# Part of VectorE's attention work moved to GpSimd, and weight loads re-timed, in a transformer-block kernel

## The reference, cut to what matters

```python
x = x + layernorm(attn(layernorm(x)))          # per head: q, k scaled to unit length
#   sim = (l2norm(q) * exp(scale)) @ l2norm(k).T; out = softmax(sim) @ v; out @ w_out + b_out
x = x + layernorm(ffn(layernorm(x)))
#   h = silu(x @ w1 * s1) * (x @ w2 * s2); h = gelu(h @ h1 * t1); h = gelu(h @ h2 * t2); h @ w3 * s3
```

## Time and profile before

| | |
|---|---|
| median of 3 runs | 1945.36 us (1936.95 to 1945.42) |
| the profiled execution | 1939.09 us, of which the span is 1937.2 us |
| TensorE, VectorE, ScalarE, GpSimd busy | 1743.2, 1203.1, 1012.1, 426.7 us |
| mean granted TensorE clock | 0.966 of full speed |

### The profile page before, as it was taken

How to read it: one execution, slowest core, us unless ns; L and a number is a source line. 1 busy time by engine, 2 the same in 40 slices (tenths; PEclk the granted TensorE clock), 3 DMA queues, 4 the chain that set the end, 5 groups by cost and what they waited for, 6 DMA issues and landing times.

```text
span 1937.2 us, 24570 instructions
## 1 busy us (share of the span) xinstructions
PE 1743.2 (90%) x8584; PEld 1443.8 (75%) x8584; DVE 1203.1 (62%) x2085; ACT 1012.1 (52%) x1349; POOL 426.7 (22%) x499
## 2 busy tenths in 40 slices
PE   4899899999899889989988984699999999999997
PEld 3677777778678778777777773587878778777876
DVE  4676786786686776776776765664443544444453
ACT  2776676777677667767766763213232331313231
POOL 3333423423323423333333320000000000000000
PEclk8999999999999999999999997799999999999999
DMA  3534544535435445455344355310000000000000
GB/s 117 120 83 116 120 98 115 115 98 121 110 100 121 109 106 132 107 116 129 87 115 111 80 137 132 112 60 2 23 2 23 14 13 23 2 23 2 24 2 22
DMA packets 71445, 152.03 MB, mean 78 GB/s; under 512 B 25968, under 2 KB 26224, under 8 KB 71280
## 3 DMA queue, kind: packets, MB, share of 16 engines
q1 hardware_dynamic: 63504, 122.34, 27.0%
q10 hardware_dynamic: 6624, 23.21, 3.8%
...
## 4 chain that ended last, share of the span: by engine, by line
PE 51%; DMA 22%; DVE 12%; issue 7%; SPq 4%; ACT 2%; POOL 1%; DVEq 0%; ACTq 0%; POOLq 0%
DMA work<-rows 13%; PE pair L1087 12%; PE pair L1088 12%; PE bank L1009 6%; DMA Dp<-work 5%; PE bank L1023 4%; PE bank L951 4%; DMA rows<-Rp 3%; DVE Pl L675 3%; PE pair L1078 3%; PE pair L1079 2%; DVE work L691 2%; SPq L252 2%; SPq L251 2%; PE bank L1116 2%
## 5 line engine op out<-in xcount | busy, mean ns | idle before, releaser
L1009 PE MATMUL bank<-Ph,V 128*128 128x512 f32 x1024 | 379.9, 412 | 103.3 <-DVE Pl L675 102.9
L1087 PE MATMUL pair<-hh,f 128*128 128x512 f32 x1024 | 405.6, 396 | 18.1 <-DVE hl L787 9.9
L468 ACT ACTIVATE P<-pair,sh 128x1024 f32<-128x1024 f32 x256 | 286.4, 1119 | 246.3 <-PE pair L993 135.6
L1088 PE MATMUL pair<-hl,f 128*128 128x512 f32 x1024 | 404.1, 395 | 0.0
L1009 PEld LDWEIGHTS bank<-Ph,V 128*128 128x128 f32 x1024 | 198.7, 194 | 176.8 <-issue 131.6
L675 DVE TENSOR_TENSOR Pl<-P,Ph 128x1024 fp32r<-128x1024 f32 x256 | 311.9, 1218 | 1.0
L513 ACT ACTIVATE hr<-pair,ct 128x512 f32<-128x512 f32 x128 | 88.2, 689 | 378.8 <-PE pair L1088 378.8
L473 ACT ACTIVATE Ph<-P 128x1024 fp32r<-128x1024 f32 x256 | 271.6, 1061 | 8.1
L1087 PEld LDWEIGHTS pair<-hh,f 128*128 128x128 f32 x1024 | 195.7, 191 | 63.3 <-issue 12.8
L1088 PEld LDWEIGHTS pair<-hl,f 128*128 128x128 f32 x1024 | 195.7, 191 | 41.3 <-issue 0.6
L358 POOL TENSOR_TENSOR rs<-ss,half 128x8 f32<-128x8 f32 x128 | 214.3, 1674 | 10.7
...
## 6 DMA issues: line engine op xcount, KB each, us to landing
stack<-turned SPq DMA_DIRECT2D x128, 384.0 KB, 4.5
stack<-turned SPq DMA_DIRECT2D x128, 256.0 KB, 5.1
...
f<-raw ACTq DMA_DIRECT2D x22, 512.0 KB, 4.9
raw<-in_h ACTq DMA_DIRECT2D x16, 512.0 KB, 5.3
xt<-in_x SPq DMA_DIRECT2D x8, 512.0 KB, 8.6
xr<-in_x SPq DMA_DIRECT2D x8, 512.0 KB, 8.8
x<-xr SPq DMA_DIRECT2D x8, 512.0 KB, 3.0
```

Of the source, the lines that this page charges most:

```text
L468: e.activation(M.P[:, i % 2, :], M.SB[i % 2][:, :], ACT.Exp, bias=M.sh[:, h:h + 1]).then_inc(S["exp"])
L1009: d = e.matmul(M.OB[:, :], v, p[:, u % 3, j * 512:(j + 1) * 512], start=jt == 0 and m == 0, stop=jt == 3 and m == 2)
L1087: e.matmul(ps, w, M.hh[src][:, k, :].bitcast(to), start=k == 0, stop=False)
L1088: d = e.matmul(ps, w, M.hl[src][:, k, :].bitcast(to), start=False, stop=k == KH - 1)
```

## The change

On GpSimd: the even head's half of `normal` (normal_even), o_low, ln1b and finish2 join o_high and head_root; normal_even, o_high and o_low of a pair stand together at the head of slot 4n + 10. On VectorE: normal_odd stands in slot 4n + 10 behind p_low; the next sequence's ln1 moves to slots 3, 4, 6, finish to 8, 9, 11, x_low to 21 and 22, and these and head_scale stand ahead of head_sums. The semaphore `on` becomes `ona` (odd) and `onb` (even). x_turn moves from slots 20, 21 to 19, 20, and `bank_plan` adds 1.5 for an x user. The load of xr moves from slot 28 to 18, the copies of weight pieces from every tenth to every eighth slot and to the head of ScalarE's slot. The loads of pieces stand in slots 246, 248, 250, and so on, one per slot, the last one in the feed-forward; the counts follow them. The second flag (all counts of a layer summed) moves from slot NU + 5 to NU + 7. norm_root moves to slot 7, ln1b to 15, out_root to 11, finish2 to 12 and 13, all on GpSimd. The diff leaves out the renamed waits in other places and the code of functions that only move.

```diff
...
@@ -98,8 +98,8 @@
             order += [(("Tk", pair_of(i)), i), (("Tq", pair_of(i)), i)]
         if quad_of(i) is not None:
             order += [(("y", 2 * quad_of(i)), i), (("y", 2 * quad_of(i) + 1), i)]
-        if b + 1 < B and i % 32 in (20, 21):
-            order.append((("x", 2 * (b + 1) + i % 32 - 20), i))
+        if b + 1 < B and i % 32 in (19, 20):
+            order.append((("x", 2 * (b + 1) + i % 32 - 19), i))
         if i == NU - 3:
             order += [(("x3", 0), i), (("x3", 1), i)]
         if i in FLAG_AT:
@@ -110,7 +110,7 @@
     for n, (user, i) in enumerate(order):
         bank = user[1] % 2 if user[0] == "x3" else 2 if i == SLOTS else min(free, key=free.get)
         plan[user] = bank, last.get(bank)
-        last[bank], free[bank] = user, i + n / len(order) + (user[0] == "qk")
+        last[bank], free[bank] = user, i + n / len(order) + {"qk": 1, "x": 1.5}.get(user[0], 0)
     return plan
 
 
...
@@ -188,20 +189,21 @@
 
 def copy_at(i):
 
-    n, r = divmod(i - 10, 10)
+    n, r = divmod(i - 10, 8)
     return n if r == 0 and 0 <= n < PIECES else None
 
 
+
+LOAD_AT = (NU - 10, NU - 8) + tuple(range(NU - 6, NU + 13))
+COUNT_AT = (NU - 7, NU - 5, NU - 3, NU - 2) + tuple(range(NU, NU + 8))
+
+
 def load_at(i):
-
-    n = i - NU + 10 if i < NU + 2 else i - NU + 9
-    return n if i != NU + 2 and 0 <= n < PIECES else None
+    return LOAD_AT.index(i) if i in LOAD_AT else None
 
 
 def count_at(i):
-
-    n = i - NU + 7
-    return n if 0 <= n < FIRST[2] else None
+    return COUNT_AT.index(i) if i in COUNT_AT else None
 
 
 MS = ((0, 1), (2,), (3,), (4,), (5,), (6,), (7,))
...
@@ -317,7 +320,7 @@
             store_x1(pb)
         if b + 1 < B and i32_ == 0:
             load_x(b + 1)
-        if live and i32_ == 28:
+        if live and i32_ == 18:
             load_xr(b)
         if i == NU - 11:
             load_xv(0)
@@ -360,10 +363,37 @@
         q.wait_ge("eq", 3)
         e.tensor_tensor(rs, rs, M.eq[:, qd, :, :, :].rearrange("p b c d -> p (b c d)"), ALU.mult).then_inc(S["rq"])
 
+    def normal_even(n):
+
+        q.wait_ge("nl", n - 1)
+        q.wait_ge(f"rb{n % 2}", 16 * (n // 2 + 1))
+        q.wait_ge("ev", 2 * n + 1)
+        e.tensor_tensor(M.on[0:64, n % 2, :], M.Ev[0:64, (2 * n) % 4, :], M.Rb[0:64, n % 2, :],
+                        ALU.mult).then_inc(S["onb"])
+
     def o_high(n):
-        q.wait_ge("on", 2 * n + 2)
+        q.wait_ge("ona", n + 1)
+        q.wait_ge("onb", n + 1)
         q.wait_ge("out", 2 * (n // 2) - 2)
         e.tensor_copy(M.nh[:, n % 2, :], M.on[:, n % 2, :]).then_inc(S["nh"])
+
+    def o_low(n):
+        q.wait_ge("nh", n + 1)
+        e.tensor_tensor(M.nl[:, n % 2, :], M.on[:, n % 2, :], M.nh[:, n % 2, :].bitcast(f32),
+                        ALU.subtract).then_inc(S["nl"])
+
+    def ln1b(b, t):
+        q.wait_ge("rd", b + 1)
+        e.tensor_scalar(M.xt[:, t, :], M.xt[:, t, :], M.mv[:, t, 0:1], M.rd[:, t:t + 1],
+                        ALU.subtract, ALU.mult).then_inc(S["xn"])
+
+    def finish2(b, t):
+        q.wait_ge("rd2", b + 1)
+        e.tensor_scalar(M.y[:, t, :], M.y[:, t, :], M.mv2[:, t, 0:1], M.rd2[:, t:t + 1],
+                        ALU.subtract, ALU.mult).then_inc(S["yn"])
+        q.wait_ge("yn", NT * b + t + 1)
+        q.wait_ge("xr", 16 * (b + 1))
+        e.tensor_tensor(M.xr[:, t, :], M.xr[:, t, :], M.y[:, t, :], ALU.add).then_inc(S["x1r"])
 
     def out_root(b):
         q.wait_ge("ve2", b + 1)
@@ -382,21 +412,36 @@
         e.dma_start(M.out[b], M.xv[:, b % 2, :, :]).then_inc(S[f"store{b % 2}"], 16)
 
     norm_root(0)
+    for t in range(NT):
+        ln1b(0, t)
     for t in range(NT + 1):
         head_root(t)
     for i in range(SLOTS):
         g, c, b, r, live = slot(i)
         i32_, pb = i % 32, i // 32 - 1
+        if i % 4 == 2 and 0 <= i // 4 - 2 < NP:
+            normal_even(i // 4 - 2)
+            o_high(i // 4 - 2)
+            o_low(i // 4 - 2)
         for u in tiles_of(i):
             head_root(u)
-        if i % 4 == 1 and 0 <= i // 4 - 2 < NP:
-            o_high(i // 4 - 2)
         if i - NU == 8:
             out_root(B - 1)
-        if 0 <= pb < B - 1 and i32_ == 9:
-            out_root(pb)
-        if b + 1 < B and i32_ == 13:
-            norm_root(b + 1)
+        if i - NU == 9:
+            for t in range(NT):
+                finish2(B - 1, t)
+        if 0 <= pb < B - 1:
+            if i32_ == 11:
+                out_root(pb)
+            if i32_ in (12, 13):
+                finish2(pb, 2 * (i32_ - 12))
+                finish2(pb, 2 * (i32_ - 12) + 1)
+        if b + 1 < B:
+            if i32_ == 7:
+                norm_root(b + 1)
+            if i32_ == 15:
+                for t in range(NT):
+                    ln1b(b + 1, t)
         if i == NU - 7:
             norm_root3(0)
     for b in range(B):
...
@@ -535,6 +581,10 @@
     split_w(7)
     for i in range(SLOTS):
         g, c, b, r, live = slot(i)
+        if copy_at(i) is not None:
+            copy_piece(copy_at(i))
+        if b + 1 < B and i % 32 == 21:
+            x_high(b + 1, 0)
         if live:
             exp(i)
             p_high(i)
@@ -551,14 +601,12 @@
         if pair_of(i) is not None:
             turn_high(pair_of(i), 1)
             turn_high(pair_of(i), 0)
-        if b + 1 < B and i % 32 in (20, 21):
-            x_high(b + 1, i % 32 - 20)
+        if b + 1 < B and i % 32 == 21:
+            x_high(b + 1, 1)
         if HEAD <= i < HEAD + 7:
             for m in MS[i - HEAD]:
                 gate(0, 0, m)
                 high0(0, m)
-        if copy_at(i) is not None:
-            copy_piece(copy_at(i))
         if load_at(i) is not None:
             load_piece(load_at(i))
         if i == NU - 3:
@@ -571,6 +619,8 @@
                 if n == 0 and m == KH - 1:
                     high0(b, m - 1)
                 gate(b, n, m)
+                if b == 0 and n == 1 and m == 0:
+                    load_piece(PIECES - 1)
                 if n == 0 and m == KH - 1:
                     high0(b, m)
                 elif n == 0 and m:
@@ -617,11 +667,6 @@
             q.wait_ge("ln1b", NT * b + NT)
             e.tensor_scalar_add(M.ve[:, :], M.mv[:, :, 1], EPS).then_inc(S["ve"])
 
...
     def x_low(b, k):
         bank = PLAN["x", 2 * b + k][0]
         q.wait_ge("xh", 2 * b + k + 1)
@@ -682,20 +727,13 @@
             q.wait_ge(f"rw{n % 2}", 16 * (n // 2))
         e.reciprocal(M.Rp[:, n % 2, :], M.Dp[:, n % 2, :]).then_inc(S["rp"])
 
-    def normal(n):
+    def normal_odd(n):
+
         q.wait_ge("nl", n - 1)
-        for odd in range(2):
-            own = slice(64 * odd, 64 * odd + 64)
-            q.wait_ge(f"rb{n % 2}", 16 * (n // 2 + 1))
-            q.wait_ge("ev", 2 * n + odd + 1)
-            e.tensor_tensor(M.on[own, n % 2, :], M.Ev[own, (2 * n + odd) % 4, :], M.Rb[own, n % 2, :],
-                            ALU.mult).then_inc(S["on"])
-
-    def o_low(n):
-        q.wait_ge("nh", n + 1)
-        q.wait_ge("out", 2 * (n // 2) - 2)
-        e.tensor_tensor(M.nl[:, n % 2, :], M.on[:, n % 2, :], M.nh[:, n % 2, :].bitcast(f32),
-                        ALU.subtract).then_inc(S["nl"])
+        q.wait_ge(f"rb{n % 2}", 16 * (n // 2 + 1))
+        q.wait_ge("ev", 2 * n + 2)
+        e.tensor_tensor(M.on[64:128, n % 2, :], M.Ev[64:128, (2 * n + 1) % 4, :], M.Rb[64:128, n % 2, :],
+                        ALU.mult).then_inc(S["ona"])
 
     def add_part(Q, half):
         n = 2 * Q + half
@@ -715,14 +753,6 @@
         if t == NT - 1:
             q.wait_ge("ln2b", NT * b + NT)
             e.tensor_scalar_add(M.ve2[:, :], M.mv2[:, :, 1], EPS).then_inc(S["ve2"])
-
...
 
     def count_piece(n):
 
@@ -808,8 +838,6 @@
 
     for t in range(NT):
         ln1(0, t)
-    for t in range(NT):
-        ln1b(0, t)
     x_low(0, 0)
     x_low(0, 1)
     split_w(0)
@@ -837,10 +865,23 @@
             split_w(4 + i)
         if i in (5, 6, 12, 13):
             split_wo(i - 5 if i < 7 else i - 10)
-        if i % 4 == 2 and 0 <= n - 3 < NP:
-            o_low(n - 3)
         if i % 4 == 3 and 0 <= n - 2 < NP:
             invert(n - 2)
+        if i % 4 == 2 and 0 <= n - 3 < NP:
+            normal_odd(n - 3)
+        if b + 1 < B and i32_ in (21, 22):
+            x_low(b + 1, i32_ - 21)
+        if tail == 8:
+            for t in range(NT):
+                finish(B - 1, t)
+        if 0 <= pb < B - 1:
+            for t in {8: (0,), 9: (1, 2), 11: (3,)}.get(i32_, ()):
+                finish(pb, t)
+        if b + 1 < B:
+            for t in {3: (0,), 4: (1, 2), 6: (3,)}.get(i32_, ()):
+                ln1(b + 1, t)
+        for u in tiles_of(i - 1) if i else []:
+            head_scale(u)
         for u in tiles_of(i):
             head_sums(u)
         if values_of(i) is not None:
@@ -848,32 +889,9 @@
         if pair_of(i) is not None:
             turn_low(pair_of(i), 1)
             turn_low(pair_of(i), 0)
-        for u in tiles_of(i - 1) if i else []:
-            head_scale(u)
```

(21 more changed lines are left out.)

26 lines of the change are left out of this document (9 added, 17 removed).

## The result

The changed kernel takes 2002.56 us (median of 4 runs, 1999.06 to 2010.2) against 1945.39 us (4 runs of the kernel before): ratio 1.0309, interval 1.0265 to 1.0353. The forecast was 1890 us, the range ended at 1930, and slower had a chance of 0.10. The profiled execution has a span of 1998.0 us against 1937.2.

A forecast was written before the change was run, and what follows sets the result against it. TensorE was taken as the busiest engine, its holes being waits for `Pl` and `xl`. Terms in us: 64 + 10 - 34 - 6 - 13 + 28 = 49 off 1939, forecast 1890 us, range 1850 to 1930.

The forecast's parts named there:

- the chain that moves to GpSimd: normal_even, cast, o_low ahead of outp: nl comes late, 4.2 us per sequence, 34 us lost; bounds 0 and 96.
- VectorE's relief, 64 + 10: Attention: less work on VectorE cuts TensorE's `Pl` waits, 64 us gained, and the granted clock gives back 10.
- Price r of a product on GpSimd: Time of a 512-element two-input product on GpSimd, not in the trace: 1.1 us taken, between 0.61 and 1.8.
- nl waits: outp's waits for nl, now made on GpSimd: near 30 us, mostly in slots 7 and 31.
- Rival 2: Pair's low half too late: products 1.8 us, p_low slips ahead of o_low each time; 62 us more, 1952 us; chance 0.10.
- Rival 4: `Pl` waits only change slot, ln1 and late head_scale delaying VectorE; 30 of 64 + 10 remain; 1934 us; chance 0.10.
- Prologue: Before the first scores: eight users in a row on one bank, 6.2 us a tile; 13 us lost, bounds 7 and 20.
- x_low: Slots 21 and 22: x_low(1) ends 0.8 us later, 7 times; 6 us lost, bounds 0 and 14.
- Handover: Attention to feed-forward: first `Pl` waits go, 26 us, plus 2 of clock; 28 gained, bounds 5 and 42; last chain stays.
- Rival 3: Handover stays bound by the weights' DMA, waits only move to slots 254 to 262; 28 lost, 1918 us; chance 0.12.
- Clock: Attention, granted clock 0.98: with fewer long holes it gives back 10 of 22 us, bounds 0 and 18.

The follow-up runs named there:

- before_loads: Kernel before with only the copies, loads, counts and second flag timed as in the changed kernel, xr in slot 18: ratio 0.9944 to the kernel before.
- late_pair: before_loads with both halves of normal and o_low in slots 4n + 10, behind p_low, still on VectorE: ratio 0.9593 to the kernel before.
- pair_only: before_loads plus the pair's end as changed: normal_even and o_low on GpSimd, normal_odd behind p_low, slot 4n + 10: ratio 0.9993 to the kernel before.
- after_slot: Changed kernel with both halves of normal and o_low back on VectorE, in the changed slot 4n + 10: ratio 0.9909 to the kernel before.
- norms_only: before_loads plus ln1b of the later sequences and finish2 on GpSimd, in their old slots: ratio 1.0000 to the kernel before.
- order_only: before_loads plus VectorE's new order alone, everything on its old engine: ratio 0.9909 to the kernel before.
- after_slot_turn: after_slot with x_turn, x_low and the bank plan also as in the kernel before: ratio 0.9665 to the kernel before.
- tuned_late: before_loads with x loaded and ln1 done one sequence earlier, plus late_pair's edit: ratio 0.9522 to the kernel before, 1855.23 us.
- pair_half: pair_only with GpSimd's product and subtraction covering 256 of 512 columns from the second quad on, output partly stale: ratio 0.9726 to the kernel before.

## Why the prediction was wrong

The step that failed most is **the chain that moves to GpSimd**, sized at 34 us. In the runs the engine of the two products costs 0.9993 - 0.9593 = 4.0%, 78 us of 1945, and the same in the changed kernel. The term looked for one consumer, outp with its wait for nl, and gave the rest of TensorE's time nothing. Behind the pair on GpSimd stands head_root of the same slot, and behind that head_scale on VectorE with all of VectorE's queue. What is queued behind the waiting instruction was asked for nl and not for rs. The traces say where the time went, from exp(0) to exp(224) (us; TensorE's waits by what ended them, and its busy time, which grows at a lower granted clock):

| run | time | `Pl` | nl | xl | bank of head_scale | TensorE busy | clock |
|---|---|---|---|---|---|---|---|
| before_loads | 1003.6 | 60.7 | 0 | 13.6 | 0 | 925.9 | 0.97 |
| late_pair | 946.2 | 14.8 | 11.3 | 1.8 | 0 | 907.6 | 0.99 |
| pair_only | 1018.8 | 28.1 | 48.0 | 1.9 | 0 | 926.2 | 0.97 |
| after_slot | 981.3 | 21.5 | 13.3 | 20.3 | 1.8 | 915.9 | 0.98 |
| changed kernel | 1044.1 | 44.2 | 26.2 | 16.5 | 14.6 | 933.2 | 0.96 |

With the two products on GpSimd the changed kernel loses 62.8 us against after_slot: 22.7 in `Pl` and 12.8 in the bank, the two that a late rs reaches through VectorE's queue, 12.9 in nl, 17.2 in busy time. (p_low itself is 10.6 us longer in all, and part of the first may be that.) On the kernel before, 72.6 us from late_pair to pair_only, the shares are others: 36.7 in nl, 13.3 in `Pl`, 18.5 in busy time. So the path through rs is the larger in the changed kernel, the one through nl in pair_only, and in both some 18 us is TensorE's own work at the lower clock.

The chain is 44 of the 109 us between -49 as predicted and +60 as measured. It doesn't turn the sign alone: with it at 34 us the kernel would still be some 16 us slower than before. The turn of x with the bank plan, the handover and the normalisations, priced wrongly or at nothing, make up most of the rest.

The parts, as predicted and as the runs give them (differences of ratios times 1945 us, each uncertain by 5 to 11 us):

| part | predicted | measured |
|---|---|---|
| pair's new slot, VectorE freed of waits (64 + 10) | -74 | -68 (before_loads to late_pair) |
| products on GpSimd | +34 | +78 (late_pair to pair_only; after_slot to changed kernel: +78) |
| ln1b, finish2 on GpSimd | 0 | +11 (norms_only) |
| VectorE's order | 0 | -7 (order_only, within its uncertainty) |
| turn of x, bank plan, prologue | +19 | +47 (after_slot to after_slot_turn) and 3.5 for ln1b(0) |
| loads, handover | -28 | -11 (before_loads) |
| sum | -49 | +54; the kernels differ by +60 |

- **VectorE's relief, 64 + 10: the size was right and the reason wrong.** The 74 came as 68 without taking a single product off VectorE. What made `Pl` late was `normal` with its wait for the spread ahead of p_low; one slot later and behind p_low it costs far less. The text had seen this ("7.6 us later") and credited engine and slot together. In the changed kernel `Pl` waits are 48.1 us and not below 15, since VectorE then waited for rs; with the products back on VectorE (after_slot) they are 22.3 up to 1130 us.
- **Price r of a product on GpSimd:** 1.1 taken, 1.29 measured (median of L371 and of L382 after; 1.26 the shortest), inside the bounds 0.61 and 1.8. The Trainium skill (GPSIMD Engine Reference, Performance versus the Vector engine) has 4497 ns for an addition of 2048 elements, from which the prediction's estimate by the page was 1.2; the trace agrees within 0.1. In pair_only, with p_low beside it, L381's median is 2.15, mean 1.86. The cast was taken at 0.61; in the changed kernel it meets a p_low in most slots, and its median is 1.52.
- **nl waits:** about 30 us forecast, 30.4 measured, by luck: 12 waits in slots 7 and 15 instead of 7 and 31, in slot 15 with finish2 ahead of the pair on GpSimd (1.8 us in the slot shown), which the prediction left out. With the products on VectorE there are 14.8 us of them already (after_slot). Rival 2 (nl too late) had the direction right, but its turning point was 83 us of waits for nl. The path through rs was in no rival. Rival 4, VectorE late in other slots, has the right symptom, put down to ln1 and not to GpSimd.
- **ln1b and finish2 on GpSimd** weren't priced. They take 1.35 and 1.64 + 0.85 us in the mean instead of VectorE's 0.41 and 0.84 (late_pair), and four ln1b of slot 15 took 5.46 us in a row (738.22, timeline after).
- **Prologue:** the plan was read rightly (all on one bank), at 6.2 us a tile; it was 7.42. 13 became 21.8; the bound was 20. exp(0) at 68.4.
- **x_low:** 6 us forecast; undoing the turn of x gave back 4.5 us per sequence, 31 in all (after_slot to after_slot_turn). The waits for xl rose only from 14.5 to 16.5 us, as forecast, but with the pair out of slot 21 they could have been 1.8 (late_pair). The bank that head_scale holds added 14.6, unforeseen, in slot 20; with the pair's products on VectorE it is 1.8, so that part belongs to the chain.
- **Handover:** 28 forecast, about nothing in the changed kernel, 11 in before_loads, about half of it before exp(224). The `Pl` waits went as forecast, 5.3 us left; the text had called the last chain latency that stays, and did not see that it and the flag's count, whose waits grew from 7.4 to 25.8 us together (before_loads), would take their place. Rival 3 has the time and not the reason.
- **Clock:** forecast to rise, it fell from 0.98 to 0.97 in attention; in late_pair and tuned_late, where the waits did go, it is 0.99 and 1.00.

What stays open: whether the 9 us of norms_only in the last slots are the same queue effect, and how the loss by GpSimd's products splits between their own length and what they and VectorE do to each other. pair_half says that two thirds follow the length; both mechanisms shrink with it. The second shows on both sides: over the whole of pair_only p_low takes 331.7 us instead of late_pair's 311.6, and the two products 211 us on GpSimd, where 128 times 1.29 would be 165. In the changed kernel p_low takes 323.1 us, the products 174 and the cast 73.0 instead of 39.1. What these us cost TensorE no run shows.
